# A two-layer decoder kernel: in its three attentions the transposes go ahead of the value product, and four exponentials run in a row

## The chip, the cores and the metric

The kernel runs on one core of one Trainium2 chip. A core has five engines with instruction queues of their own, which meet only through semaphores: TensorE (PE: matmuls and transposes into PSUM; its weight loads are listed as PEld), VectorE (DVE), ScalarE (ACT), GpSimd (POOL) and SyncE (SP, transfers). The metric is the device time of one execution in microseconds, lower is better.

## What is computed

A decoder of two layers on x of 8 batches x 128 tokens x 128 features, with a context of 8 x 77 x 128. Six blocks follow each other, each added to its input and normalised. Blocks 1, 2 and 5 are attentions with 16 heads of 8 features; they are what the change touches:

```python
x = _layernorm(x + _L0_attn_ref(x, ...))            # attention 1: own keys, 128 of them
x = _layernorm(x + _L0_xattn_ref(x, ctx_1024, ...)) # attention 2: 77 keys of the context
x = _layernorm(x + _L0_ffn_ref(x, ...))             # mixture of experts
x = _layernorm(x + _L1_attn_ref(x, ...))            # state space model and small attention
x = _layernorm(x + _L1_xattn_ref(x, ctx_1024, ctx_1024, mask_1x1xSxS2_bk1, ...))  # attention 5: 77 keys, masked
x = _layernorm(x + _L1_ffn_ref(x, ...))             # experts with full capacity

scores = jnp.einsum('bhqd,bhkd->bhqk', Q, K) / jnp.sqrt(jnp.float32(D_K))
scores = jnp.where(mask, -jnp.inf, scores)
attn_w = jax.nn.softmax(scores, axis=-1)
out = jnp.einsum('bhqk,bhkd->bhqd', attn_w, V)
```

## The kernel before

The three attentions use the same code, with an object `Attention` each (`at1`, `at2`, `at5`) that holds the semaphores and says which PSUM bank a step uses. The work goes batch by batch (B = 8); the 16 heads lie in four groups of 32 rows (G = 4), and a group's four heads are told apart by keys that are zero outside their head. One batch takes these steps:

- `scores(b)` (PE, L1572): query by keys for the four groups, into four banks; attention 5 writes the mask first (L1565).
- `maximum(b, g)` (DVE, L1064), four of them: the largest score of each query and head.
- `remainder(b, k)` (DVE, L1074), two of them: splits the maxima into parts that bf16 holds exactly.
- `flips(i)` (PE): up to four things into one bank: the output projection of batch i-3 (L1636), in attention 2 for i = 1 to 4 the transpose of a late query (L1640), the transpose of the maxima of batch i+1 (L1643), the transpose of the normalised values of batch i-2 (L1646). It waits for `part_ready`, that is both remainders of batch i+1, and for `normed`.
- the flips' copy (ACT, L707) takes the maxima and the values to SBUF; in attention 2 a second one (L709) takes the late query.
- `shifted(b)` (PE): keys by query once more, transposed (L1596), minus the flipped maxima (L1603); in attention 5 the masks come first (L1589). It waits until all its four banks are read, among them that of the first maximum of batch b+1, and for the flips' copy.
- `exponentials(b, groups)` (ACT, L690), four of them.
- `weigh(b)` (PE, L1625): values by exponentials, with the sums as an extra column.
- copy of the weighted values (ACT, L701), their transposes back (PE, L1674), which I call turns, then on DVE `inverse` (L1029; in attention 5 also L1033) and `normalise` (L1041).
- `residual` (DVE, L1017) adds the projection, `statistics` and `apply` (L1004) normalise, with one power on POOL between them. In attention 2 DVE also scales a late query (L1205) at the end of turns 0 to 3.

The order of each engine is written out by hand. PE's turn i is `shifted(i)`, `weigh(i-1)`, `flips(i)`, `scores(i+2)`, turns of i-1. ACT's turn i is exponentials 0 and 1 of i, copy of the weighted values of i-1, flips' copy of i, exponentials 2 and 3 of i. DVE's turn i is `residual(i-3)`, maximum 0 of i+2, `inverse(i-1)`, maximum 1, `normalise(i-1)`, maxima 2 and 3, remainder 0, `apply`, remainder 1, `statistics`. Seven banks go round in a ring (`RING_BANKS`) for scores, `flips` and `shifted`; the order of their uses is `SLOTS`. `between`, `middle`, `within` and `opening` are pieces of the neighbouring blocks that are set into chosen turns.

Of the kernel before, what the change touches and what calls it, by code (L numbers as in the profile page):

```python
# [30 lines left out]
G = 4  # L31
# [78 lines left out]
BURSTS = [("max", 0), ("flip", -1), ("max", 1)]  # L110
for _i in range(B):
    BURSTS += [("exp", _i), ("flip", _i)] + ([("max", _i + 2)] if _i + 2 < B else [])
SLOTS = [(what, i, g) for what, i in BURSTS for g in range(1 if what == "flip" else G)]
PLACE = {slot: n for n, slot in enumerate(SLOTS)}


class Attention:


    def __init__(self, sem, name, nk, scale, kM, V, Wo, XB, Xout, masked=False, late=None):  # L120
# [5 lines left out]
        self.late = late  # L126
        self.scores_ready = sem(f"{name}_scores_ready")
# [17 lines left out]
    def bank(self, what, i, g=0):  # L145

        if what == "flip" and i >= B:
            return 5 if i == B + 1 else 7
        return RING_BANKS[PLACE[what, i, g] % len(RING_BANKS)]

# [10 lines left out]
    def wait_bank(self, pe, what, i, g=0):  # L161
# [6 lines left out]
        place = PLACE[what, i, g] - len(RING_BANKS)  # L168
        if place >= 0:
            before, k, slot = SLOTS[place]  # L170
# [28 lines left out]
def _build(nc, ctx, a, out):  # L199
# [37 lines left out]
    mask8 = sb("mask8", [128, NC], U8); maskneg = sb("maskneg", [128, NC], BF16); maskrep8 = sb("maskrep8", [128, 4, NC], U8); maskrep = sb("maskrep", [128, 4, 2, NC], BF16); negkey = sb("negkey", [128, J, NC], BF16); first32 = sb("first32", [128, T], BF16); eye32 = sb("eye32", [128, 32])  # L237
# [247 lines left out]
    def _(pool):  # L485
# [23 lines left out]
        P_.memset(first32[:], 0.0)  # L509
# [144 lines left out]
    def _(act):  # L654
# [27 lines left out]
        def attention_scalar(at, between):  # L682
# [10 lines left out]
            for i in range(-1, B + 4):  # L693
                if 0 <= i < B:
                    exponentials(i, (0, 1))
# [7 lines left out]
                if i < B + 2:  # L703

                    lo, hi = (0 if i + 1 < B else T), (2 * T if i >= 2 else T)
                    act.wait_ge(at.flipped_ready, i + 2)
                    A_(flipped[:, i % 2, lo:hi], PS[:, at.bank("flip", i), lo:hi], ACT.Copy).then_inc(at.flipped_copied, 1)  # L707
                if at.late and 1 <= i <= HB:
                    A_(qT[:, HB + i - 1, :], PS[:, at.bank("flip", i), 3 * T:4 * T], ACT.Identity,  # L709
                       scale=gb2[:, 0:1], bias=gb2[:, 1:2]).then_inc(at.late, 1)  # L710
                if 0 <= i < B:
                    exponentials(i, (2, 3))
# [220 lines left out]
    def _(dve):  # L933
# [123 lines left out]
        def attention_vector(at, between, middle={}, ending=last_batches):  # L1057
# [19 lines left out]
            for i in range(-2, B):  # L1077
# [4 lines left out]
                if ahead:  # L1082
                    maximum(i + 2, 0)
                if done:
                    inverted = inverse(at, n)
                if ahead:
                    maximum(i + 2, 1)
# [1115 lines left out]
```

## Time and profile before

| | |
|---|---|
| median of 3 executions | 397.94 us (396.94 to 400.10) |
| the profiled execution | 400.24 us, span 398.4 us between its first and last instruction |
| mean granted clock of TensorE | 0.98 |
| busy share of the span | PE 90%, DVE 69%, PEld 60%, ACT 53%, POOL 37% |
| attention 1, about 14 to 66 us | PE busy 45.35 us of 52, DVE 41.36, ACT 32.02 |
| attention 2, about 74 to 115 us | PE busy 36.54 us of 41, DVE 24.08, ACT 24.32 |
| attention 5, about 253 to 303 us | PE busy 43.49 us of 50, DVE 30.41, ACT 21.63 |

The profile is one execution, times in microseconds from the first instruction. A matmul is listed from its start to its modelled end, and matmuls overlap, so a step's length is read from start to start. The granted clock is a share of full speed: 1.00 is 2.4 GHz, 0.50 is 1.2 GHz. A bracket at the end of a timeline row says how long the engine sat idle before it, and what ended that.

### The profile page before, as it was taken

What the parts mean: (1) busy time and instruction counts of PE and PEld (TensorE: products, weight loads), DVE (VectorE), ACT (ScalarE), POOL (GpSimd) and SP (SyncE); (2) the same over time, 40 slices, a digit from 0 to 9 for tenths busy, and PEclk for the clock granted to TensorE, in tenths of its full rate; (3) what the DMA queues carried; (4) which work ended last, traced back from release to release, by engine and by line L of the source; (5) the groups of instructions that cost most, each with busy time, mean ns of one, the idle gap of its engine ahead of it and who ended that gap; (6) DMA issues with size and microseconds to landing.
All of it is one profiled execution on the core that took longest, in us unless ns stands there. A gap on an engine that the chain in (4) does not pass through costs nothing.

```text
span 398.4 us, 10075 instructions
## 1 busy us (share of the span) xinstructions
PE 358.2 (90%) x4034; PEld 240.3 (60%) x4039; DVE 275.5 (69%) x712; ACT 211.1 (53%) x427; POOL 145.5 (37%) x128
## 2 busy tenths in 40 slices
PE   4988898798998989999999999699898999999991
PEld 2555565566675746566767667366664566666671
DVE  6877978736757877789899995755566445444546
ACT  2855468655674345999999951144354521222110
POOL 6939952481441420038889980200112000000002
PEclk9999999969999989999999999999999999999997
DMA  6335100000000030212223240620000000000001
GB/s 176 83 66 30 11 3 1 4 2 2 4 2 0 2 18 3 69 56 86 105 91 112 87 57 2 213 106 3 3 7 0 2 0 0 2 1 0 2 0 53
DMA packets 36810, 14.57 MB, mean 37 GB/s; under 512 B 26452, under 2 KB 34061, under 8 KB 36765
## 3 DMA queue, kind: packets, MB, share of 16 engines
q1 hardware_dynamic: 35466, 13.23, 13.7%
q10 hardware_dynamic: 1299, 0.71, 0.6%
q8 instruction: 32, 0.52, 0.6%
q14 instruction: 13, 0.11, 0.1%
HBM read 12.65 MB, written 0.57 MB: 33 GB/s over the span
## 4 chain that ended last, share of the span: by engine, by line
PE 78%; DVE 10%; ACT 6%; issue 4%; POOL 2%; POOLq 0%; DVEq 0%
PE PS L2045 10%; PE PS L2130 7%; PE PS L2134 7%; PE PS L2161 7%; PE PS L1625 6%; PE PS L1596 6%; PE PS L2032 5%; PE PS L1572 4%; PE PS L1532 4%; DVE mxp L1064 3%; PE PS L1538 2%; PE PS L1636 2%; PE PS L1837 2%; PE PS L1527 2%; PE PS L1589 1%
## 5 line engine op out<-in xcount | busy, mean ns | idle before, releaser
L690 ACT ACTIVATE att<-PS 103x384 f32<-103x384 f32 (+1 forms) x96 | 45.1, 525 | 43.7 <-PE PS L1603 43.7
L1064 DVE TENSOR_REDUCE mxp<-PS 128x4 f32<-128x308 f32 (+1 forms) x96 | 48.2, 536 | 21.0 <-PE PS L1572 20.9
L929 ACT ACTIVATE kM<-PS 128x512 f32<-128x512 f32 x32 | 19.1, 597 | 55.4 <-PE PS L2130 55.4
L533 POOL TENSOR_TENSOR rstd<-ve,neg_half 128x4 f32<-128x4 f32 x6 | 6.1, 1025 | 103.9 <-DVE ve L959 103.9
L539 POOL TENSOR_TENSOR rstd<-ve,neg_half 128x1 f32<-128x1 f32 x24 | 14.2, 593 | 77.3 <-DVE ve L1000 77.3
L1471 DVE TENSOR_TENSOR big<-kM,PS 128x512 f32<-128x512 f32 x32 | 21.9, 687 | 27.3 <-PE PS L2134 26.0
L1387 DVE TENSOR_TENSOR_SCAN big<-big,PS 128x768 f32<-128x768 f32 x22 | 38.2, 1746 | 2.5 <-PE PS L2032 2.2
L2130 PE MATMUL PS<-xT,V 128*128 128x512 f32 x64 | 33.0, 597 | 1.1 <-DVE xT L1459 0.8
L2134 PE MATMUL PS<-xT,V 128*128 128x512 f32 x64 | 32.7, 592 | 0.0
L2161 PEld LDWEIGHTS PS<-big 128*128 128x128 f32 x256 | 29.7, 192 | 3.3 <-issue 3.3
L2161 PE MATMUL PS<-big 128*128 128x128 f32 x256 | 29.7, 275 | 0.0
L895 ACT ACTIVATE att<-big,BT 128x256 f32<-128x256 f32 x64 | 27.1, 493 | 0.0
L1492 DVE SCALAR_TENSOR_TENSOR R<-PS,aff,R 128x128 f32<-128x128 f32 x56 | 15.8, 344 | 11.2 <-PE PS L2161 11.2
L578 POOL TENSOR_TENSOR hr<-hvar,half_bh 77x32 f32<-77x32 f32 (+1 forms) x5 | 22.0, 4424 | 1.8 <-DVE hvar L986 1.8
L1596 PE MATMUL PS<-qT,kM 32*103 32x128 f32 x384 | 18.5, 301 | 3.6 <-DVE mxp L1064 2.6
L2134 PEld LDWEIGHTS PS<-xT,V 128*128 128x128 f32 x64 | 12.2, 190 | 15.3 <-issue 14.8
L1625 PE MATMUL PS<-att,V 103*32 103x128 f32 x512 | 19.0, 285 | 1.2 <-issue 0.9
L1387 DVE TENSOR_TENSOR_SCAN untransposed<-untransposed,PS 128x768 f32<-128x768 f32 x10 | 17.4, 1744 | 3.5 <-PE PS L2032 3.4
L881 ACT ACTIVATE big<-big,Aneg 128x760 f32<-128x760 f32 x22 | 19.6, 915 | 0.0
L2032 PE MATMUL PS<-ident,att 128*128 128x128 f32 x128 | 19.3, 273 | 0.4 <-ACT att L895 0.4
L1518 PE MATMUL PS<-negsel,identb 128*128 128x512 bf16 x49 | 14.8, 424 | 4.7 <-DVE negsel L1116 4.4
L2130 PEld LDWEIGHTS PS<-xT,V 128*128 128x128 f32 x64 | 11.5, 190 | 12.5 <-issue 11.2
(363 smaller groups left out, 832.8 us busy)
## 6 DMA issues: line engine op xcount, KB each, us to landing
kM<-Cdram SPq DMA_DIRECT2D x6, 384.0 KB, 3.3
XH<-Cdram SPq DMA_DIRECT2D x5, 384.0 KB, 3.3
xT<-Cdram SPq DMA_DIRECT2D x5, 384.0 KB, 3.5
V<-in_L_ffn_Wg SPq DMA_DIRECT2D x1, 1024.0 KB, 5.5
V<-in_L_ffn_Wu SPq DMA_DIRECT2D x1, 1024.0 KB, 8.1
out_x<-X SPq DMA_DIRECT2D x2, 256.0 KB, 2.3
ctxN<-in_ctx ACTq DMA_DIRECT2D x1, 308.0 KB
X<-in_x ACTq DMA_DIRECT2D x1, 256.0 KB, 3.8
```

The costliest lines, as they stand in the source:

```text
L578: P_.tensor_tensor(out=hr1[0:NC, n], in0=hvar[0:NC, n], in1=half_bh[0:NC, 0:n.stop - n.start], op=ALU.pow)\
L690: A_((PTk if at.packed else PT)[0:at.kt, i % 2, g], bank4(at.bank("exp", i, g), at.kt)[:, 0:nt, :], ACT.Exp, scale=at.scale).then_inc(at.e ...
L895: ins = A_(scaled[s % 2][k], duT[:, k, :], ACT.Identity, scale=BT[:, k, s:s + 1])
L1064: V_.tensor_reduce(mxp[:, b % 3, g, 0:J], PS[:, at.bank("max", b, g), 0:J * nk].rearrange("p (j k) -> p j k", j=J), axis=AX.X, op=ALU.max) ...
L1387: V_.tensor_tensor_scan(hst[m % NHS], dA[m % NDA], dBu[m % NDB], 0.0, ALU.mult, ALU.add)\
L1596: M_(tile(b, g, k), keys, qT[rows(g), b, :], start=not at.masked, stop=False)
L1625: ins = M_(PS[32 * u:32 * u + 32, at.out_bank(b), k * T:(k + 1) * T], values[0:at.kt, lo:lo + VW], weights, start=(x == 0), stop=(x == 1))
L2032: ins = nc.tensor.transpose(dBu[n % NDB][:, 128 * k:128 * (k + 1)], scaled[s % 2][k][:, 128 * h:128 * (h + 1)], ident[:])
L2045: ins = M_(y_piece(h, lo, hi), ident[:], hC[n % NHC][:, lo:hi], start=False, stop=(n // NH == DS - 1 and (h, lo) != (0, 512)))
L2130: M_(PS[:, n % 2, :], Wg6[:, e, i * 128:(i + 1) * 128], half(xT, c), start=True, stop=True)\
L2134: M_(PS[:, 2 + n % 2, :], Wu6[:, e, i * 128:(i + 1) * 128], half(xT, c), start=True, stop=True)\
L2161: ins = M_(PS[:, 4 + (2 * e + c) % 4, b4 * D:(b4 + 1) * D], hidE[e % 2][:, i, b * T:(b + 1) * T], Wd6[:, NI * e + i, :], start=(i == 0), s ...
```

## The change

The order within a turn changes on three engines, for all three attentions alike. PE: for i < 8 `flips(i)` stands ahead of `weigh(i-1)`, and `scores(i+2)` behind it; from i = 8 on the order is as before, and ahead of each `between` a wait for `residual_ready` is added. ACT: the four exponentials of a batch run in a row, then the flips' copy (and the late query's), then the copy of the weighted values; from i = 8 on as before. DVE: maximum 1 stands ahead of `inverse`. The masks of attention 5 for the first 32 queries are written 32 columns wide instead of 128, `first32` is that much narrower, and its memset on POOL goes. The slots are computed per attention, with the same content.

```diff
--- before.py
+++ after.py
@@ -107,11 +107,14 @@
 
 
 RING_BANKS = [0, 1, 2, 3, 4, 5, 7]
-BURSTS = [("max", 0), ("flip", -1), ("max", 1)]
-for _i in range(B):
-    BURSTS += [("exp", _i), ("flip", _i)] + ([("max", _i + 2)] if _i + 2 < B else [])
-SLOTS = [(what, i, g) for what, i in BURSTS for g in range(1 if what == "flip" else G)]
-PLACE = {slot: n for n, slot in enumerate(SLOTS)}
+
+
+def slots():
+
+    bursts = [("max", 0), ("flip", -1), ("max", 1)]
+    for i in range(B):
+        bursts += [("exp", i), ("flip", i)] + ([("max", i + 2)] if i + 2 < B else [])
+    return [(what, i, g) for what, i in bursts for g in range(1 if what == "flip" else G)]
 
 
 class Attention:
@@ -124,6 +127,8 @@
         self.kt = KT if self.packed else T
         self.Wo, self.XB, self.Xout, self.masked = Wo, XB, Xout, masked
         self.late = late
+        self.slots = slots()
+        self.place = {slot: n for n, slot in enumerate(self.slots)}
         self.scores_ready = sem(f"{name}_scores_ready")
         self.max_ready = sem(f"{name}_max_ready")
         self.part_ready = sem(f"{name}_part_ready")
@@ -146,7 +151,7 @@
 
         if what == "flip" and i >= B:
             return 5 if i == B + 1 else 7
-        return RING_BANKS[PLACE[what, i, g] % len(RING_BANKS)]
+        return RING_BANKS[self.place[what, i, g] % len(RING_BANKS)]
 
     def out_bank(self, b):
 
@@ -165,9 +170,9 @@
             if i == B + 2:
                 self.wait_flip_read(pe, B)
             return
-        place = PLACE[what, i, g] - len(RING_BANKS)
+        place = self.place[what, i, g] - len(RING_BANKS)
         if place >= 0:
-            before, k, slot = SLOTS[place]
+            before, k, slot = self.slots[place]
             if before == "flip":
                 self.wait_flip_read(pe, k)
             else:
@@ -234,7 +239,7 @@
     untransposed = sb("untransposed", [128, 12 * D])
     W5 = untransposed[:, 0:4 * D].rearrange("p (i n) -> p i n", i=4)
     W5T = sb("W5T", [128, 4, D])
-    mask8 = sb("mask8", [128, NC], U8); maskneg = sb("maskneg", [128, NC], BF16); maskrep8 = sb("maskrep8", [128, 4, NC], U8); maskrep = sb("maskrep", [128, 4, 2, NC], BF16); negkey = sb("negkey", [128, J, NC], BF16); first32 = sb("first32", [128, T], BF16); eye32 = sb("eye32", [128, 32])
+    mask8 = sb("mask8", [128, NC], U8); maskneg = sb("maskneg", [128, NC], BF16); maskrep8 = sb("maskrep8", [128, 4, NC], U8); maskrep = sb("maskrep", [128, 4, 2, NC], BF16); negkey = sb("negkey", [128, J, NC], BF16); first32 = sb("first32", [128, 32], BF16); eye32 = sb("eye32", [128, 32])
     maskf = sb("maskf", [128, NC]); nmasked = sb("nmasked", [128, 1]); anykey = sb("anykey", [128, 1])
     gate3 = sb("gate3", [E0, D]); gate3T = sb("gate3T", [128, E0])
     down3 = untransposed[:, 4 * D:8 * D].rearrange("p (i n) -> p i n", i=4)
@@ -506,7 +511,6 @@
         affine(ident[:], ALU.not_equal, [[-1, 128]]).then_inc(const_ready, 1)
         pool.wait_ge(const_ready, 1)
         P_.memset(identb[:], 0.0)
-        P_.memset(first32[:], 0.0)
         P_.memset(after[:], 0.0)
         P_.memset(earlier[:], 0.0)
         P_.memset(mxp[:], 0.0).then_inc(event("mxp_zero"), 1)
@@ -692,7 +696,19 @@
 
             for i in range(-1, B + 4):
                 if 0 <= i < B:
-                    exponentials(i, (0, 1))
+                    exponentials(i, range(G))
+                def flips_out():
+                    if i < B + 2:
+
+                        lo, hi = (0 if i + 1 < B else T), (2 * T if i >= 2 else T)
+                        act.wait_ge(at.flipped_ready, i + 2)
+                        A_(flipped[:, i % 2, lo:hi], PS[:, at.bank("flip", i), lo:hi], ACT.Copy).then_inc(at.flipped_copied, 1)
+                    if at.late and 1 <= i <= HB:
+                        A_(qT[:, HB + i - 1, :], PS[:, at.bank("flip", i), 3 * T:4 * T], ACT.Identity,
+                           scale=gb2[:, 0:1], bias=gb2[:, 1:2]).then_inc(at.late, 1)
+
+                if i < B:
+                    flips_out()
                 if 0 <= i - 1 < B:
 
                     act.wait_ge(at.pv_done, i)
@@ -700,16 +716,8 @@
                         act.wait_ge(at.out_ready, i - 1)
                     A_(outT[:], PS[:, at.out_bank(i - 1), 0:2 * T].rearrange("p (k t) -> p k t", k=2), ACT.Copy)\
                         .then_inc(at.outT_copied, 1)
-                if i < B + 2:
-
-                    lo, hi = (0 if i + 1 < B else T), (2 * T if i >= 2 else T)
-                    act.wait_ge(at.flipped_ready, i + 2)
-                    A_(flipped[:, i % 2, lo:hi], PS[:, at.bank("flip", i), lo:hi], ACT.Copy).then_inc(at.flipped_copied, 1)
-                if at.late and 1 <= i <= HB:
-                    A_(qT[:, HB + i - 1, :], PS[:, at.bank("flip", i), 3 * T:4 * T], ACT.Identity,
-                       scale=gb2[:, 0:1], bias=gb2[:, 1:2]).then_inc(at.late, 1)
-                if 0 <= i < B:
-                    exponentials(i, (2, 3))
+                if i >= B:
+                    flips_out()
                 if i in between:
                     between[i]()
 
@@ -1081,10 +1089,9 @@
                     residual(at, r)
                 if ahead:
                     maximum(i + 2, 0)
+                    maximum(i + 2, 1)
                 if done:
                     inverted = inverse(at, n)
-                if ahead:
-                    maximum(i + 2, 1)
                 if done:
                     normalise(at, n, inverted)
                 if i in middle:
@@ -1153,7 +1160,7 @@
             V_.tensor_scalar(maskrep[:], maskrep8[:].rearrange("p c (o k) -> p c o k", o=1).to_broadcast([128, 4, 2, NC]), MASKED,
                              None, ALU.mult)
             step(V_.tensor_reduce(eye32[:], ident[:].rearrange("p (g r) -> p r g", g=G), axis=AX.X, op=ALU.add))
-            V_.tensor_copy(first32[:, 0:32], eye32[:])
+            V_.tensor_copy(first32[:], eye32[:])
             step(V_.tensor_reduce(nmasked[:], mask8[:], axis=AX.X, op=ALU.add))
             step(V_.tensor_scalar(anykey[:], nmasked[:], float(NC), None, ALU.is_lt))
 
@@ -1582,11 +1589,11 @@
 
                 if at.masked:
                     for c in range(4):
-                        q = slice(32 * c, 32 * c + 32) if c else slice(0, T)
+                        q = slice(32 * c, 32 * c + 32)
                         for k, lo in enumerate(at.tiles):
                             for g in range(G):
                                 keys = maskrep[rows(g), c].rearrange("p r n -> p (r n)")[:, lo % NC:lo % NC + KT]
-                                M_(tile(b, g, k)[:, q], keys, first32[rows(g), 0:q.stop - q.start], start=(c == k == 0), stop=False)
+                                M_(tile(b, g, k)[:, q], keys, first32[rows(g), 0:32], start=(c == k == 0), stop=False)
                 for k, lo in enumerate(at.tiles):
                     for g in range(G):
                         if at.packed:
@@ -1658,16 +1665,18 @@
                     shifted(i)
                 if i == 0:
                     opening[4]()
+                if i < B:
+                    flips(i)
                 if 0 <= i - 1 < B:
                     weigh(i - 1)
-                if i < B + 3:
+                if i + 2 < B:
+                    scores(i + 2)
+                if B <= i < B + 3:
                     flips(i)
                 if i in middle:
 
                     pe.wait_ge(at.exp_ready, G * min(i, B))
                     middle[i]()
-                if i + 2 < B:
-                    scores(i + 2)
                 if 0 <= i - 1 < B:
                     pe.wait_ge(at.outT_copied, i)
                     for k in range(2):
@@ -1678,6 +1687,7 @@
                 if i in between:
 
                     pe.wait_ge(at.exp_ready, G * B)
+                    pe.wait_ge(at.residual_ready, B - 3)
                     between[i]()
 
             if last_wait:
```

## Rows read from the trace of the kernel before

**Rows 1.** Waits of PE, all of the span: us in total, times, longest.

```profile
PE PS L1596 <- DVE mxp L1064: 6.8, 10, 0.9
```

**Rows 2.** Chain of waits, attention 1: start, us, what held the end.

```profile
20.78 0.14 issue
...
29.43 1.16 PE PS L1572 x8
30.59 0.70 DVE mxp L1064
```

**Rows 3.** Timeline, one turn of attention 1: start, us, engine, line, out<-in, idle before.

```profile
30.59 0.69 DVE L1064 TENSOR_REDUCE mxp<-PS 128x4 f32<-128x512 f32 x1 [0.64 <-PE PS L1572]
...
33.02 1.08 PE L1625 MATMUL PS<-att,big 128*32 128x128 f32 x32
...
33.41 0.38 DVE L1074 TENSOR_TENSOR mxp<-mxp 128x16 f32<-128x16 f32 x2
...
34.04 0.33 PE L1643 MATMUL PS<-ident,mxp 128*128 128x128 f32 x1
```

**Rows 4.** Timeline of PE, attention 1: first and last scores, last turns.

```profile
24.53 1.14 PE L1572 MATMUL PS<-big,qT 32*128 32x512 f32 x8
...
50.39 1.14 PE L1572 MATMUL PS<-big,qT 32*128 32x512 f32 x8
...
53.98 1.08 PE L1625 MATMUL PS<-att,big 128*32 128x128 f32 x32
...
56.26 0.50 PE L1596 MATMUL PS<-qT,big 32*128 32x128 f32 x8 [0.26 <-ACT flipped L707]
...
57.75 1.08 PE L1625 MATMUL PS<-att,big 128*32 128x128 f32 x32
...
61.27 0.49 PE L1636 MATMUL PS<-Wo,flipped 128*128 128x128 f32 x2
```

**Rows 5.** Timeline of ACT, attentions 1 and 2: two exponentials, a copy.

```profile
54.12 1.08 ACT L690 ACTIVATE att<-PS 128x512 f32<-128x512 f32 x2 [2.26 <-PE PS L1603]
55.12 0.38 ACT L701 ACTIVATE outT<-PS 128x256 f32<-128x256 f32 x1
...
104.33 0.87 ACT L690 ACTIVATE att<-PS 103x384 f32<-103x384 f32 x2 [1.52 <-PE PS L1603]
```

**Rows 6.** Timeline, attention 2, turns 1, 3 and 4.

```profile
79.40 0.28 DVE L1205 TENSOR_TENSOR qc<-qc,hr 128x128 f32<-128x128 f32 x1
...
79.46 1.94 PE L1625 MATMUL PS<-att,V 103*32 103x128 f32 x32
...
93.02 0.29 DVE L1017 TENSOR_TENSOR R<-XB,PS 128x128 f32<-128x128 f32 x1 [2.20 <-ACT qT L709]
...
95.03 1.08 PE L1625 MATMUL PS<-att,V 103*32 103x128 f32 x32
...
96.10 0.29 DVE L1205 TENSOR_TENSOR qc<-qc,hr 128x128 f32<-128x128 f32 x1
```

**Rows 7.** Timeline, attention 5, turn 2.

```profile
269.97 0.39 DVE L1074 TENSOR_TENSOR mxp<-mxp 128x16 f32<-128x16 f32 x2
...
270.09 1.08 PE L1625 MATMUL PS<-att,V 103*32 103x128 f32 x32
```

**Rows 8.** Groups by line and shape: mask matmuls; busy us, mean ns.

```profile
L1589 PE MATMUL PS<-first,maskrep 32*103 32x32 bf16 x288 | 4.8, 192 | 0.0
L1589 PE MATMUL PS<-first,maskrep 32*103 32x128 bf16 x96 | 3.1, 227 | 2.7 <-DVE mxp L1064 1.9 <-ACT flipped L707 0.8
```

**Rows 9.** Timeline, the start.

```profile
2.28 0.20 POOL L509 MEMSET first<- 128x128 bf16 x1
...
3.18 0.29 DVE L1114 TENSOR_REDUCE headmask<-ident 128x4 f32<-128x128 f32 x1 [3.18 <-POOL mxp L512]
```

**Rows 10.** Busy time by stretch: length; PE, PEld, DVE, ACT, POOL; clock; DMA share, GB/s.

```profile
80.00:85.00 5.00, 4.87 (x56) 2.89 (x52) 1.46 (x5) 2.12 (x6) 5.00 (x3) 0.50 0.00 0
253.00:258.00 5.00, 3.40 (x51) 1.33 (x51) 2.89 (x14) 0.71 (x2) 1.01 (x1) 1.00 1.04 346
```

## Prediction

> **What bounds the kernel now.** I read the granted clock first (0.98 on the one core), then PE's waits, then the chain of waits, then the timeline of PE, DVE and ACT through the three attentions. The change touches nothing else but one memset at the start.
>
> PE's waits: inside the attentions the longest total is `shifted` (L1596) waiting for the maxima of DVE, 6.8 us in 10 waits, none over 0.9 [rows 1]. The chain shows why. In attention 1 it goes round as scores (PE), first maximum (DVE, 30.59, 0.70 us), `shifted`, `weigh`, `flips`, scores again [rows 2]. So per batch PE is the bound, with one hole in which the first maximum is made. A second loop runs beside it: scores, all four maxima and two remainders on DVE, `flips`, scores. Its length shows in the timeline of attention 1: the first maximum of a batch starts at 30.59, the second remainder ends at 33.41+0.38 = 33.79, and `flips`, which needs it, starts at 34.04. Between 33.02 and 34.04 PE does `weigh` [rows 3]. The reader is to see that `weigh` is what PE does while DVE finishes the remainder: `shifted` ends, `weigh` starts at 33.02, the remainder is 0.77 us from its end.
>
> **The change, part by part.**
>
> *1. `flips(i)` ahead of `weigh(i-1)` on PE.* `flips(i)` transposes the maxima of batch i+1, so it waits for both remainders of that batch. Scores of batch i+1 are issued one turn earlier, behind the same `weigh`. Now the order is scores, `shifted`, `flips`, `weigh`, scores; the two loops are no longer side by side: the DVE loop gets `weigh` in series. Queued behind the waiting `flips` on PE are `weigh(i-1)`, scores(i+2) and the transposes of the weighted values; DVE waits for scores, ACT for `weigh`.
>
> Attention 1, from scores to scores: 1.16 us from the scores' start (29.43) to the first maximum (30.59) and 0.14 us from a remainder's end to PE's start [rows 2]; 3.20 us from the first maximum to the end of the second remainder, 0.33 us of transposes, 1.01 us of `weigh` (33.02 to 34.04) [rows 3]: 5.84 us. The first of five such steps has no inverse and no normalisation between its maxima (0.29 us less), the last has an `apply` between its remainders (0.14 us more). Sum 5 x 5.84 - 0.15 = 29.05 us. Before, scores(2) started at 24.53 and scores(7) at 50.39, so the same five steps took 25.86 us [rows 4]. **+3.2 us.**
>
> Attention 2 has shorter maxima (308 columns), but in turns 1 to 4 `flips` also turns a late query, which DVE scales behind the remainders. Here I count the wait itself: end of DVE's last piece, plus latency, less the end of `shifted` (where `weigh` starts now), less 0.32 us for the projection that `flips` does first from turn 3. Turn 1: 79.40+0.28+0.06-79.46 = 0.28 us; turn 4, the largest: 96.10+0.29+0.06-95.03-0.32 = 1.1 us [rows 6]. The same sum gives 0.30, 0.50 and 0.50 for turns 2, 3 and 5; together 2.7 us. Something comes back: at 93.02 DVE's `residual` starts 2.20 us idle, held by ACT's late query copy, and holds the first maximum back [rows 6]. With `flips` 1.01 us before the scores that hold is gone, 0.4 us in each of two turns. **+1.9 us.**
>
> Attention 5 has its mask matmuls in `shifted`, which makes `shifted` longer and gives DVE more time. Turn 2: the remainder ends at 269.97+0.39 = 270.36, `weigh` starts at 270.09, so the wait is 0.41 us [rows 7]; turns 3, 4 and 5 by the same sum 0.09, 0 and 0.23. **+0.7 us.**
>
> *2. Four exponentials in a row on ACT, then the flips' copy, then the weighted values' copy.* In the middle of an attention this is covered: the next consumer of either copy stands behind scores, 1 us or more later. The cover is gone at the last two turns, where no scores follow. Turn 6: the copy of the weighted values starts when `weigh(5)` is done, which itself waited; in attention 1 that is 2.5 us behind the end of `shifted` (wait 1.05, transposes 0.31, then 1.14 as from `weigh` at 53.98 to the copy at 55.12), then 0.38 for the copy, 0.14 to PE, and an estimated 0.37 for two transposes (by the 0.33 of one in [rows 3]): `shifted(7)` starts 3.4 us behind, against 56.26-53.98 = 2.28 before [rows 4, 5]: +1.1 us. Attention 2 by the same sum +0.9, attention 5 +0.6. Turn 7: four exponentials take 1.08+2x0.49 = 2.1 us in attention 1 and 0.87+2x0.38 = 1.6 in the others [rows 5]; then the copies, the transposes, then `weigh(7)`, which stands behind them on PE: 4.2 us from the end of `shifted(7)` to the next `flips`, against 61.27-57.75 = 3.52 before [rows 4]: +0.7; in the two others 3.7 against 3.3: +0.4 each. **+4.1 us over the three.**
>
> *3. Masks in 32 columns instead of 128 (attention 5).* The wide form takes 227 ns on average, the narrow 192 [rows 8]. In a batch 12 wide ones run four abreast, so three rounds of 0.035 us: 0.1 us a batch. From below it is worth nothing, if weight loads set the pace; from above 0.15 us, three whole rounds of the 0.05 us at which the 48 go. It counts only in turns where `flips` does not wait for DVE, some three of eight: **-0.3 us** (0 to -0.5).
>
> *4. Memset of `first32` gone from POOL.* DVE's first instruction waits for POOL's `mxp` memset until 3.18 [rows 9]; the memset removed stands before it and takes 0.20 us with some overlap. **-0.15 us** (0 to -0.2).
>
> *5. At nothing:* the second maximum ahead of the inverse (same DVE work; it covers a later transpose of the weighted values), the extra wait for `residual_ready` ahead of `between` (the `flips` before it needs a normalisation which DVE does behind that residual), the slots made per attention (same order, same banks). Without its cover each costs at most one DVE piece, 0.3 us, a few times: under 1 us together.
>
> Sum: 3.2 + 1.9 + 0.7 + 4.1 - 0.3 - 0.15 = **+9.4 us**. The profiled execution took 400.24 us, so it would take 409.7. The median of the runs shown is 397.94, 2.3 us below it; I put the sum on the median: **407.4 us**.
>
> **TensorE's clock.** The row of 80 to 85 us shows the granted clock at 0.50, the lower level of 1.2 GHz; from 253 to 258, with PE busy only 3.40 us of 5, it stayed at 1.00, the level of 2.4 GHz [rows 10]. At the lower level `weigh` takes 1.94 instead of 1.08 us [rows 6]; 5 us at half rate cost up to 2.5 us. The changed attention 1 would have PE busy about 4.35 of 5.84 us, 3.7 of 5, above a window that kept the clock, so I count nothing for it and make it a rival. The Trainium skill, "TensorE: Matmul & The Clock Gate", section "A second HAM failure mode: psum-queue depth-cycling", says that short idle gaps between groups of matmuls can make the clock swing between its levels. By that page each swing would add 2.5 us to the sum; by the row of 253 to 258 it need not come.
>
> **Rivals.**
> *A lower clock on top.* One more stretch as in [rows 10], 2.5 us, gives 409.9; two give 412.4. For it: attention 2 already has such a stretch, and the change adds holes of 0.3 to 1.1 us to every turn. Against: the idler window at 253 us kept the clock. The stretch of before may also vanish, 2.5 us the other way: 404.9.
> *Only the ends cost.* If in the middle turns DVE's loop is shorter than its rows say, parts 2 to 4 remain: 4.1-0.45 = +3.7, 401.6 us. Against: the parts of that loop are all data dependences, measured in place.
> *Not slower.* PE idles before `shifted` anyway, and `weigh` next to scores could fill this hole. The place is the wait of `flips` for the second remainder. It decides the other way only if the remainder ends before `shifted` does: 0.77 us earlier in attention 1, 0.3 to 1.1 in attention 2, 0.4 in attention 5. Then the masks (eight times 0.1), the held residual (0.8) and the memset remain, with the ends covered: -1.7, 396.2 us. For it: in attention 5 three of five waits are under 0.25 us. Against: DVE cannot begin before scores end, and nothing in the change moves scores forward.
>
> **Chances.** Forecast 0.62 (its own range 404.9 to 409.9: the old stretch gone, or a longer one), lower clock on top 0.17, only the ends 0.13, not slower 0.08. A measurement of this kernel tells about 1% from no change, so 394.0 and 401.9 are the bounds. Slower: forecast, lower clock and over half of "only the ends", 0.87. Faster: a small part of "not slower", 0.03. Same: the rest, 0.10. The range of 8 in 10 goes from "only the ends", 401.8, to a first added stretch at the lower clock and part of a second, 412.5.
>
> **What would show it.** In the profile of the changed kernel: PE's waits should name `flips` (the transpose of `mxp`) waiting for DVE's remainder, some 0.6 to 0.9 us a turn in attention 1, where before there was none; from scores to scores about 5.85 us in attention 1; `shifted` still waiting for the first maximum; the transposes of the weighted values at turns 6 and 7 waiting for ACT's copy. It would be wrong if `flips` starts without a wait, if scores to scores stays near 5.2 us in attention 1, or if the attentions are longer in stretches at clock 0.50 instead of by waits.

## The result and the profile after

| | |
|---|---|
| median after, 4 executions | 411.58 us (408.97 to 411.79) |
| median before beside it, 4 executions | 397.76 us (396.94 to 400.10) |
| ratio after to before, 95% interval | 1.0294 (1.0253 to 1.0334): slower |
| the profiled execution after | 411.61 us, span 409.8 us (before 400.24, 398.4) |
| busy share of the span | PE 88%, DVE 68%, PEld 59%, ACT 51%, POOL 36% |

The forecast was 407.4 us, with 401.8 to 412.5. The ratio stands for 11.7 us on 397.76; the two medians lie 13.8 us apart, and the profiled execution after has a late start of 1.96 us, which the last section shows. The forecast's sum was 9.4. Three executions in the sets below were in a second, much slower state (1974.85 us of the changed kernel with ACT as before, 609.26 and 606.60 us of before): the ratios leave them out, the medians count them. PE's busy time is nearly the same (360.9 us, before 358.2): what is added is waiting. The waits of PE in the changed kernel (us in total, times, longest):

```profile
PE PS L1603 <- DVE mxp L1072: 7.4, 13, 0.9
PE PS L1650 <- DVE mxp L1082: 5.4, 10, 1.0
...
PE PS L1683 <- ACT outT L717: 3.4, 6, 0.7
PE PS L1647 <- DVE qc L1212: 3.1, 4, 1.1
```

Lines have moved: L1603 is `shifted` (before L1596), L1650 the transpose of the maxima in `flips` (L1643), L1647 that of the late query (L1640), L1683 the turns (L1674), L1072 `maximum`, L1082 `remainder`. The reader is to see that the wait of `shifted` for the first maximum is nearly as it was (6.8 us in [rows 1], 7.4 now), and that three waits are new or were small: `flips` for the second remainder, 5.4 us, and for the late query, 3.1 us, and the turns for ACT's copy, 3.4 us.

Where they lie is in the timeline of the changed kernel: one turn of attention 1, its end, a mask block of attention 5, and at the top three rows from the start of the kernel.

```profile
3.03 0.29 DVE L1121 TENSOR_REDUCE headmask<-ident 128x4 f32<-128x128 f32 x1 [3.03 <-POOL mxp L516]
...
4.31 0.87 DVE L962 BATCH_NORM_STATS2 st<-X 128x6 f32<-128x128 f32 x4 [0.20 <-DMA X<-in_x]
...
8.27 1.12 PE L1534 MATMUL PS<-ident,XH 128*128 128x128 f32 x4 [0.45 <-DVE XH L974]
...
31.91 1.14 PE L1579 MATMUL PS<-big,qT 32*128 32x512 f32 x8
...
33.12 1.29 DVE L1072 TENSOR_REDUCE mxp<-PS 128x4 f32<-128x512 f32 x2 [1.22 <-PE PS L1579]
...
34.33 0.25 DVE L1037 RECIPROCAL rs<-PS 128x16 f32<-128x16 f32 x1
...
34.61 0.29 DVE L1049 TENSOR_TENSOR oN<-PS,rs 128x128 f32<-128x128 f32 x1
...
36.13 0.38 DVE L1082 TENSOR_TENSOR mxp<-mxp 128x16 f32<-128x16 f32 x2
...
36.66 0.30 PE L1650 MATMUL PS<-ident,mxp 128*128 128x128 f32 x1 [1.03 <-DVE mxp L1082]
...
37.00 1.08 PE L1632 MATMUL PS<-att,big 128*32 128x128 f32 x32
38.01 1.14 PE L1579 MATMUL PS<-big,qT 32*128 32x512 f32 x8
...
61.21 1.08 PE L1632 MATMUL PS<-att,big 128*32 128x128 f32 x32
62.79 0.44 PE L1683 MATMUL PS<-ident,outT 128*128 128x128 f32 x2 [0.50 <-ACT outT L717]
63.16 0.50 PE L1603 MATMUL PS<-qT,big 32*128 32x128 f32 x8
...
67.36 0.44 PE L1683 MATMUL PS<-ident,outT 128*128 128x128 f32 x2 [0.52 <-ACT outT L717]
67.73 1.08 PE L1632 MATMUL PS<-att,big 128*32 128x128 f32 x32
68.74 0.49 PE L1643 MATMUL PS<-Wo,flipped 128*128 128x128 f32 x2
...
278.34 0.76 PE L1596 MATMUL PS<-first,maskrep 32*103 32x32 bf16 x48 [0.39 <-DVE mxp L1072]
278.92 0.48 PE L1603 MATMUL PS<-qT,kM 32*103 32x128 f32 x8
```

In [rows 3] PE did `weigh` while DVE finished the remainder. Here PE stands still for 1.03 us until 36.66, and `weigh` follows at 37.00. From scores (31.91) to scores (38.01) 6.10 us pass.

### The profile page after: what moved, and what is told of

It is laid out like the page before. It is cut to its first block, busy times and chain, and to the rows that moved or that the text cites. A ratio compares the mean times of both kernels' runs of the same rounds, so it can differ in the third digit from the quotient of the medians.

```text
span 409.8 us, 10069 instructions
## 1 busy us (share of the span) xinstructions
PE 360.9 (88%) x4039; PEld 240.5 (59%) x4039; DVE 278.2 (68%) x712; ACT 208.6 (51%) x427; POOL 145.7 (36%) x127
## 4 chain that ended last, share of the span: by engine, by line
PE 71%; DVE 15%; ACT 6%; issue 5%; POOL 1%; DMA 1%; POOLq 0%; DVEq 0%
PE PS L2055 10%; PE PS L2140 7%; PE PS L2144 7%; DVE mxp L1072 7%; PE PS L2171 7%; PE PS L1632 5%; PE PS L1579 5%; PE PS L2042 5%; PE PS L1539 4%; PE PS L1545 3%; PE PS L1603 2%; PE PS L1534 2%; PE PS L1847 2%; ACT att L694 1%; PE PS L1650 1%
## 5 line engine op out<-in xcount | busy, mean ns | idle before, releaser
L694 ACT ACTIVATE att<-PS 103x384 f32<-103x384 f32 (+1 forms) x96 | 42.6, 529 | 57.7 <-PE PS L1610 57.7
L1072 DVE TENSOR_REDUCE mxp<-PS 128x4 f32<-128x308 f32 (+1 forms) x96 | 47.5, 542 | 26.9 <-PE PS L1579 26.8
L1603 PE MATMUL PS<-qT,kM 32*103 32x128 f32 x384 | 17.8, 291 | 2.9 <-DVE mxp L1072 2.7
L1525 PE MATMUL PS<-negsel,identb 128*128 128x512 bf16 x54 | 16.5, 436 | 4.3 <-DVE negsel L1123 4.3
L2042 PEld LDWEIGHTS PS<-ident,att 128*128 128x128 f32 x128 | 15.3, 141 | 5.7 <-issue 3.6
```

Source lines behind the costliest of these rows:

```text
L694: A_((PTk if at.packed else PT)[0:at.kt, i % 2, g], bank4(at.bank("exp", i, g), at.kt)[:, 0:nt, :], ACT.Exp, scale=at.scale).then_inc(at.e ...
L1072: V_.tensor_reduce(mxp[:, b % 3, g, 0:J], PS[:, at.bank("max", b, g), 0:J * nk].rearrange("p (j k) -> p j k", j=J), axis=AX.X, op=ALU.max) ...
L1603: M_(tile(b, g, k), keys, qT[rows(g), b, :], start=not at.masked, stop=False)
L2042: ins = nc.tensor.transpose(dBu[n % NDB][:, 128 * k:128 * (k + 1)], scaled[s % 2][k][:, 128 * h:128 * (h + 1)], ident[:])
```

## Where the time went, and eleven experiments

Each kernel is read by the same six lengths from its timeline of PE: for each attention the **middle** (from the start of scores(2) to the start of scores(7), five steps) and the **end** (from there to the start of the projection in `flips(8)`, the part in which no scores follow). In attention 5 both are read from the first product of query and keys, behind the masks that scores write first. A star marks a length into which a stretch at a lower granted clock falls.

| kernel | median us | ratio (95%) | middles 1, 2, 5 | ends 1, 2, 5 |
|---|---|---|---|---|
| before | 397.76 | | 25.86, 24.96*, 26.93 | 10.88, 9.31, 10.50 |
| after | 411.58 | 1.0294 (1.0253 to 1.0334) | 29.61, 25.53, 27.85 | 12.64, 10.60, 11.46 |
| PE order alone | 409.63 | 1.0234 (1.0187 to 1.0281) | 28.87, 26.16, 27.43* | 12.19, 10.66, 11.30 |
| ACT order alone | 401.52 | 1.0032 (1.0011 to 1.0052) | 26.01, 22.41, 27.20 | 12.35, 10.20, 11.41 |
| DVE order alone | 399.11 | 1.0000 (0.9965 to 1.0036) | 26.29, 22.46, 27.20 | 10.92, 9.31, 10.51 |
| masks and memset alone | 399.73 | 1.0007 (0.9980 to 1.0033) | 25.85, 22.37, 26.86* | 10.89, 9.46, 10.46 |
| after, split flips | 404.89 | 1.0123 (1.0021 to 1.0225) | 26.59, 22.62, 28.01* | 12.35, 10.36, 11.53 |
| after, DVE as before | 409.47 | 1.0246 (1.0150 to 1.0342) | 28.87, 24.79, 27.65 | 12.45, 10.42, 11.34 |
| after, ACT as before | 411.63 | 1.0309 (1.0212 to 1.0406) | 29.61, 26.90, 26.81* | 12.38, 10.84, 11.41 |
| after, once more | 411.21 | 1.0293 (1.0211 to 1.0374) | 31.20*, 25.52, 27.58 | 12.64, 10.60, 11.46 |
| after, ends as before | 407.69 | 1.0214 (1.0174 to 1.0254) | 29.61, 25.52, 27.11* | 10.92, 9.31, 10.46 |
| split flips, ACT as before | 400.72 | 1.0047 (1.0014 to 1.0081) | 26.58, 24.39*, 27.12 | 11.39, 9.83, 10.96 |
| split flips, ends as before | 399.24 | 1.0006 (0.9977 to 1.0036) | 26.58, 22.62, 27.39 | 10.92, 9.31, 10.46 |

The ratios are against before in executions made beside them; its median there was 399.81 us for the four with one part alone, 401.03 for split flips to "once more", and 399.67 for the last three. Attention 2's middle of before is 22.4 us without its stretch at the lower clock, by the three kernels that do not touch PE's order. With that, after against before is 3.75 + 3.13 + 0.92 us in the middles and 1.76 + 1.29 + 0.96 in the ends, 11.8 us. That agrees with the ratio's 11.7.

**One part alone.** The first four kernels are before with one part of the change. In the diffs here and below, "..." marks a cut and the comments are added.

*PE's order* (with the added wait for `residual_ready`):

```diff
+                if i < B:
+                    flips(i)
                 if 0 <= i - 1 < B:
                     weigh(i - 1)
-                if i < B + 3:
+                if i + 2 < B:
+                    scores(i + 2)
+                if B <= i < B + 3:
                     flips(i)
...
-                if i + 2 < B:
-                    scores(i + 2)
...
```

> The kernel before with PE's order alone changed (flips ahead of weigh, the added wait for the residual). Theory A, the loop over DVE gets weigh in series: flips waits for the second remainder; from scores(2) to scores(7) in attention 1 about 29 us instead of 25.9, shifted(7) 3.4 us behind the end of shifted(6) instead of 2.3 since weigh(5) is late; +7 to +9 us in all. Theory B, the copies that ACT does later are the cause: from scores to scores as before, +0 to +2 us. Theory C, TensorE's clock at its lower level is the cause: scores to scores as before outside a stretch at granted clock 0.50.

```profile
PE PS L1643 <- DVE mxp L1074: 3.9, 9, 0.8
PE PS L1676 <- ACT outT L701: 2.5, 5, 0.5
PE PS L1640 <- DVE qc L1205: 1.9, 3, 0.9
```

These are waits of PE in that kernel; L1643 and L1640 are `flips`, which in before waited for the maxima 0.5 us in all. 409.63 us, 9.8 more than the 399.81 beside it and more than the 7 to 9 expected: this part alone brings most of the loss. In attention 1 the middle took 28.87 us, 3.01 more than before; the prediction's sum had 3.2. The three ends are 3.46 us longer too, with ACT's order untouched.

*ACT's order:*

```diff
-                    exponentials(i, (0, 1))
+                    exponentials(i, range(G))
...
+                if i < B:
+                    flips_out()     # flips' copy, late query's copy
                 if 0 <= i - 1 < B:  # then the copy of the weighted values
...
```

> The kernel before with ACT's order alone changed (four exponentials, flips' copy, weighted values' copy). Theory A: in the middle turns nearly covered, 0.1 to 0.3 us a turn, since the transposes of the weighted values wait for the copy; in the last two turns shifted(7) about 3.3 us behind the end of shifted(6) in attention 1 instead of 2.3, then 4.2 to the next flips instead of 3.5; +3 to +5 us in all. Theory B: nearly all of the loss is here, +9 us or more. Theory C: about 0 outside a stretch at clock 0.50.

The end of attention 1 in that kernel, timeline of ACT and PE:

```profile
54.55 2.06 ACT L690 ACTIVATE att<-PS 128x512 f32<-128x512 f32 x4 [2.62 <-PE PS L1607]
56.47 0.42 ACT L701 ACTIVATE flipped<-PS 128x256 f32<-128x256 f32 x1
56.73 0.43 ACT L713 ACTIVATE outT<-PS 128x256 f32<-128x256 f32 x1
...
57.22 0.44 PE L1678 MATMUL PS<-ident,outT 128*128 128x128 f32 x2 [1.09 <-ACT outT L713]
```

The copy of the weighted values comes behind four exponentials and a copy, and the turns wait 1.09 us for it. The middles stay within 0.3 us of before's; the three ends are 3.27 us longer. The ratio, 1.0032, shows only part of that. The ten executions of this kernel had a mean granted clock of 0.990 on average, the 25 of before beside them 0.985. Where the clocks are alike, at 0.989 and 0.990, four executions of it took 401.16 to 402.76 us and six of before 397.60 to 398.53, on average 401.74 and 398.12: 3.6 us, where the six lengths add up to 3.7.

*DVE's order:* `maximum(i + 2, 1)` ahead of `inverse`.

> The kernel before with DVE's order alone changed (second maximum ahead of the inverse). If inverse and normalise, now back to back, wait for each other, the time from the first maximum to the end of the second remainder grows from 3.20 to about 3.4 us in attention 1; flips has some 0.1 us of slack there, so 0 to +1 us in all. If the order is free, 0.

399.11 us, no difference that can be told; the middle of attention 1 is 0.43 us longer. The chain from the first maximum to the end of the second remainder grew: 30.65 to 34.04 in its timeline, 3.39 us, against 3.20 in [rows 3]; in before's PE order `weigh` covers most of that.

*Masks 32 columns wide, memset gone:*

> The kernel before with the masks 32 columns wide and the memset of first32 gone. If a wide mask matmul costs 0.035 us more and PE is the bound, -0.1 us in each of eight turns of attention 5 and -0.15 us at the start: -0.5 to -1 us. If weight loads set the pace of the masks and the start waits for the load of x, 0.

399.73 us, no difference. The mask matmuls now take 202 ns on average; [rows 8] had 192 and 227.

**Which wait of `flips` it is.** Split flips: the changed kernel with only the projection and the transpose of the normalised values ahead of `weigh`, and the two transposes that need DVE's late results behind it.

```diff
                 if i < B:
-                    flips(i)
+                    flips(i, True, i + 1 >= B)   # projection, normalised values
                 if 0 <= i - 1 < B:
                     weigh(i - 1)
+                if i + 1 < B:
+                    flips(i, False, True)        # late query, maxima
                 if i + 2 < B:
                     scores(i + 2)
```

> The changed kernel, but of flips only the projection and the transpose of the normalised values go ahead of weigh; the late query and the transpose of the maxima, which wait for DVE's remainders, go behind it. Theory A (the DVE loop has weigh in series): scores(2) to scores(7) in attention 1 back from 29.6 to about 26 us, PE's wait for the remainder gone, what is left is ACT's late copies in the last two turns; some 7 us less than the changed kernel, +3 to +5 us over the kernel before. If it is the position of flips as such or the order of ACT and DVE: still +9 us or more.

One turn of attention 1, timeline of PE:

```profile
33.06 0.33 PE L1649 MATMUL PS<-ident,oN 128*128 128x128 f32 x1
33.31 1.08 PE L1632 MATMUL PS<-att,big 128*32 128x128 f32 x32
34.33 0.33 PE L1656 MATMUL PS<-ident,mxp 128*128 128x128 f32 x1
34.59 1.14 PE L1579 MATMUL PS<-big,qT 32*128 32x512 f32 x8
```

No row has a bracket: nothing waits. `weigh` starts at 33.31 and the maxima are there when it ends. The middle of attention 1 falls from 29.61 to 26.59 us, that of attention 2 from 25.53 to 22.62; attention 5's (28.01) can't be compared, as the stretch at a lower clock falls into it. So the cost of the middles is the wait for DVE ahead of `weigh`, and not `flips` ahead of `weigh` as such. The ends stay long, and the time is 404.89 us.

**DVE's order under the changed PE order.** The changed kernel with `inverse` back between the two maxima:

> The changed kernel with DVE's old order (inverse between the first and second maximum). In the changed kernel first maximum to end of second remainder takes 3.39 us in attention 1, against 3.20 before; here it should be 3.20 again, and since flips waits for it, every step from scores to scores is 0.15 to 0.2 us shorter: -2 to -2.5 us against the changed kernel over 15 turns. If the inverse then has to wait for the late transposes of the weighted values, less than that or 0.

```profile
31.41 0.69 DVE L1072 TENSOR_REDUCE mxp<-PS 128x4 f32<-128x512 f32 x1 [1.22 <-PE PS L1580]
32.01 0.25 DVE L1037 RECIPROCAL rs<-PS 128x16 f32<-128x16 f32 x1
32.18 0.63 DVE L1072 TENSOR_REDUCE mxp<-PS 128x4 f32<-128x512 f32 x1
32.72 0.28 DVE L1049 TENSOR_TENSOR oN<-PS,rs 128x128 f32<-128x128 f32 x1
32.91 1.28 DVE L1072 TENSOR_REDUCE mxp<-PS 128x4 f32<-128x512 f32 x2
34.23 0.39 DVE L1082 TENSOR_TENSOR mxp<-mxp 128x16 f32<-128x16 f32 x2
```

409.47 us, 2.1 less than after, but 1.7 less than the changed kernel once more (411.21), which ran beside it, and the intervals of the two ratios overlap: by the times alone it isn't clear of the noise. The lengths show it. The chain is 31.41 to 34.62, 3.21 us, where after has 33.12 to 36.51, 3.39. Attention 1's middle gives back 0.74 us, attention 2's 0.74, attention 5's 0.20, the ends 0.49: 2.2 us.

**ACT's order under the changed PE order.** The changed kernel with ACT as before:

> The changed kernel with ACT's old order (two exponentials, weighted values' copy, flips' copy, two exponentials). Theory A: scores to scores as in the changed kernel, about 29.6 us for the five in attention 1; in the last turn 0.3 us instead of 0.6 over before; -1 us or so against the changed kernel, +10 us over before. Theory B: most of the loss gone.

411.63 us: nothing comes back. The ends give 0.07 us, and attention 2's middle is 1.37 us longer. (Attention 5's is 1.04 us shorter, 0.68 of it in the last step, where the changed kernel has a stall without a wait; see below.) This timeline of it shows why attention 2's grew:

```profile
105.28 0.38 ACT L705 ACTIVATE outT<-PS 128x256 f32<-128x256 f32 x1 [2.23 <-PE PS L1628]
105.56 0.38 ACT L711 ACTIVATE flipped<-PS 128x256 f32<-128x256 f32 x1
105.83 0.46 ACT L713 ACTIVATE qT<-PS,gb 128x128 f32<-128x128 f32 x1
...
107.35 0.48 PE L1599 MATMUL PS<-qT,kM 32*103 32x128 f32 x8 [1.03 <-DVE mxp L1068]
```

ACT copies the weighted values first, so it waits for `weigh`, which now comes late. Behind it stand flips' copy and the late query's copy (105.83; in after 104.05), DVE's `residual` waits for the latter, the first maximum for `residual`, and `shifted` 1.03 us for the maximum (0.38 in after). ACT's new order takes this away; under the new PE order it costs nothing.

**The clock at the start.** The changed kernel unaltered, once more:

> The changed kernel unchanged, once more. In its first profile TensorE's clock was low in the first 15 us, which put scores(2) of attention 1 at 26.5 instead of 24.5 us; the kernel before had its low stretch in attention 2. If where such a stretch falls is chance, this profile has it elsewhere or not at all, with scores to scores in attention 1 the same 29.6 us; if the change puts it at the start, scores(2) is at 26.5 again.

411.21 us. Its scores(2) started at 24.61, where the first profile of the changed kernel has 26.49 and before 24.53 [rows 4]. The expectation puts the late start down to a low clock; the rows of the first profile show the clock at 1.00 there (last section). This profile lost the time elsewhere. Busy time by stretch (columns as in [rows 10]):

```profile
35.00:40.00 5.00, 4.39 (x48) 2.31 (x50) 1.12 (x2) 1.70 (x5) 5.00 (x2) 0.66 0.58 33
```

Two steps of attention 1 took 7.01 and 6.65 us instead of 6.10 and 5.99, which makes its middle 31.20.

**The ends.** The changed kernel with turns 6 and 7 in the order of before on PE and ACT:

```diff
-                if i < B:
+                if i < B - 2:
                     flips(i)
...
-                if B <= i < B + 3:
+                if B - 2 <= i < B + 3:
                     flips(i)
```

On ACT, likewise, `range(G)` becomes `(0, 1)` in these turns, and exponentials 2 and 3 come last.

> The changed kernel, with turns 6 and 7 of each attention (where no scores follow) in the order of before on PE and ACT: weigh ahead of flips, copy of the weighted values and flips' copy between the exponentials. Theory A (the order of the last two turns itself costs, as the prediction's part 2 says): from the start of the last scores of attention 1 to the first scores of attention 2 it goes from 20.16 back to 18.4-18.7 us, attention 5's end by about 1.0, attention 2's by about 1.0; together -3.5 to -4 against the changed kernel, some 407.5-408. Theory B (the end is longer because the middle turns hand it a later state, as it was 19.70 with the PE order alone too): it stays at 19.7 or more and the time at 410.5-411.5.

407.69 us, 3.9 less than after. The ends are 10.92, 9.31 and 10.46 us, those of before, and the middles of attentions 1 and 2 are unchanged (attention 5's is 0.74 us shorter, without the stall in its last step). So the order of the last two turns itself costs; the middle hands it nothing.

Split flips with ACT's order as before:

> The changed kernel with only the projection and the transpose of the normalised values ahead of weigh (maxima and late query behind it), and ACT's order as before. If ACT's order is what is left of the loss in the kernel with the split flips (404.89), the end of attention 1 goes from 19.86 to 18.4-18.7 us and the time to that of before, within 1 us of it. If the PE order of the last two turns (flips whole ahead of weigh) lengthens the ends by itself, the end of attention 1 stays near 19.7 and the time 3-4 us above before.

400.72 us, 1.1 above the 399.67 beside it; but at clocks of 0.989 to 0.991 five executions took 400.62 us on average and three of before 397.73, 2.9 less. The ends are still 1.49 us longer than before's, 0.5 each: in turn 7, where no maxima are left, `flips` still goes whole ahead of `weigh(6)`.

Split flips, with turns 6 and 7 as before:

> The changed kernel with split flips in turns 0 to 5 and the order of before in turns 6 and 7 on PE and ACT; ACT's row of four exponentials stays in the middle turns. Both costs named (wait ahead of weigh, ends) are gone: the time of before within 1 us, 0 to -0.5 if the narrow masks' 0.03 us a turn can be seen. If the middle turns of ACT's order cost by themselves, 1-2 us above before, seen in the steps from scores to scores (26.0 in attention 1 with ACT's order alone, 25.86 before).

399.24 us against 399.67, ratio 1.0006 (0.9977 to 1.0036): both costs are gone as far as the ratio tells. The lengths still have 0.72 us in attention 1's middle, of which DVE's order alone had 0.43, about 0.2 in attention 2's and 0.46 in attention 5's; and where the clocks are alike it is slower: at 0.993 and 0.994 four executions took 398.17 us on average, four of before 396.84, 1.3 us less. Nothing of the change is left that helps, and a version that beats before did not come out of it.

## Point by point

**The bound and the main term: right.** *1, attention 1* was +3.2 us; PE's order alone measured +3.01, and with DVE's new order 3.75. `flips` waits for the remainder (0.55, 1.03, 0.43, 0.53, 0.66 and 0.66 us in turns 1 to 6), as the wait was predicted; scores to scores was to be 5.84 us and is 5.98 to 6.12 in four of five steps.

*1, attention 2* was +1.9 us and is +3.13. The waits in the changed kernel are 0.53, 1.00, 0.49, 1.12 and 0.43 us, 3.57 in all, where the prediction had 0.28, 0.30, 0.50, 1.1 and 0.50:

```profile
87.30 0.30 PE L1647 MATMUL PS<-ident,qc 128*128 128x128 f32 x1 [0.53 <-DVE qc L1212]
...
92.37 0.30 PE L1647 MATMUL PS<-ident,qc 128*128 128x128 f32 x1 [1.00 <-DVE qc L1212]
...
97.45 0.33 PE L1647 MATMUL PS<-ident,qc 128*128 128x128 f32 x1 [0.49 <-DVE qc L1212]
...
103.18 0.33 PE L1647 MATMUL PS<-ident,qc 128*128 128x128 f32 x1 [1.12 <-DVE qc L1212]
...
108.22 0.33 PE L1650 MATMUL PS<-ident,mxp 128*128 128x128 f32 x1 [0.43 <-DVE mxp L1082]
```

The two that are far off are turns 1 and 2, read from [rows 6] and beside them, where PE ran at the lower clock. There `shifted`, whose end stands in the sum, took 1.34 us (78.12 to 79.46 in the timeline of before) and 1.83 (84.11 to 85.94); at full clock it takes 1.09 (89.13 to 90.22). The differences, 0.25 and 0.74 us, are nearly what the two waits are longer than predicted, 0.25 and 0.70. The starts in the timeline of before:

```profile
78.12 0.48 PE L1596 MATMUL PS<-qT,kM 32*103 32x128 f32 x8 [0.72 <-DVE mxp L1064]
...
84.11 0.77 PE L1596 MATMUL PS<-qT,kM 32*103 32x128 f32 x8
...
85.94 1.08 PE L1625 MATMUL PS<-att,V 103*32 103x128 f32 x32
...
89.13 0.48 PE L1596 MATMUL PS<-qT,kM 32*103 32x128 f32 x8 [0.53 <-ACT att L690]
...
90.22 1.08 PE L1625 MATMUL PS<-att,V 103*32 103x128 f32 x32
```

That turns 3 to 5 agree is in part luck: DVE's new order, counted at nothing, is in the measured waits, and with DVE as before they are 0.30, 0.94 and 0.24 us. DVE's order has 0.74 us in this middle; with DVE as before it is 24.79, +2.4. The hold of `residual` went as predicted, though ACT's new order is needed for it.

*1, attention 5* was +0.7 and is +0.92, in part by luck: the first four steps are 1.27 us longer, and the last is 0.34 shorter because before's has a stall of 0.94 us within `weigh` that no wait explains (at 287.49). The changed kernel has such stalls too, of 0.19 us (274.46) and 0.27 (298.24). What they come from is open, and the term is not settled more closely.

*2, the ends* were +4.1 us over the three and are +4.01, by attention 1.76 (predicted 1.8), 1.29 (1.3) and 0.96 (1.0). The size is right, in part by luck: 0.49 us of it goes with DVE's new order, which the term did not have. The name is half right: the prediction counted the late `weigh(5)` in turn 6, but filed the whole term under ACT's order. PE's order alone costs 3.46 us, ACT's alone 3.27, both 4.01; with ACT as before nearly all of it stays. They are two ways of delaying the same copy of the weighted values: it comes behind `weigh`, which PE holds back for the remainder, or behind two more exponentials.

*3, masks* were -0.3 us. The block of 48 mask matmuls takes 0.58 us (278.34 to 278.92) and took 0.61 (273.31 to 273.92 in the timeline of before): 0.03 us a batch, not 0.10, near the bound "worth nothing, if weight loads set the pace".

*4, memset* was -0.15 us. DVE does start at 3.03 instead of 3.18 [rows 9], but its first `BATCH_NORM_STATS2` then waits 0.20 us for the load of x, and starts at 4.31 (4.19 before). It is worth nothing.

**The step that was mis-sized** is *5*, the edits at nothing: "the second maximum ahead of the inverse" was to be the same DVE work. It adds 0.18 us to the chain from the first maximum to the second remainder, and part 1 had just put that chain on the path: 2.2 us by the lengths of the kernel with DVE as before, where all of *5* was bounded at "under 1 us together". The term was costed with the cover of the old order, which the change itself removes.

**The rivals.** "Not slower" and "only the ends" are out: `flips` waits 14 times for DVE. "A lower clock on top" did not come as told. The stretches of 30 to 65 us and 80 to 120 us of the changed kernel are at 1.00 throughout, though PE waits in each turn. The Trainium skill, "TensorE: Matmul & The Clock Gate", section "A second HAM failure mode: psum-queue depth-cycling", tells of a kernel whose clock swung between its two levels because PE idled briefly between groups of matmuls; the profile of the changed kernel shows none of that in its attentions, that of "once more" one stretch at 0.66, and before, without these gaps, one at 0.50 [rows 10]. Holes in the turns alone do not bring a lower clock here.

**Why the number was low.** The measured lengths give 11.8 us where the sum had 9.4. Attention 1 is 0.55 us over its term, attention 2 1.23, attention 5 0.22, the ends 0.09 under, and masks and memset, 0.45 in the sum, gave next to nothing. DVE's order is 1.5 us of that in attentions 1 and 2. The median stands another 1.8 us above 407.4 + 2.4. That is about the late start of 1.96 us in the profiled execution (411.61 us), which no term has; two of the other three took 411.54 and 411.79 us, the third 408.97, and whether those two started late as well is not shown.

## What to carry over

Before an instruction is moved ahead of another on an in-order engine, ask what it waits for: it may be the work that it passes that covers the wait, and then only the parts with early operands can move (split flips). Once a chain has lost its cover, cost every edit on that chain again, also those that were free. Look at the turns where the pipeline drains by themselves: here they were a third of the loss, and two edits that each delay the same copy don't add up.

## What the hardware showed that was not expected

A dependent DVE instruction right behind its source started later here than an independent one. Behind the reciprocal, a maximum starts 0.17 us later (32.01 to 32.18), the normalisation that waits for it 0.28 us later (34.33 to 34.61 in after's timeline); two maxima in a row take 1.21 us, 1.14 with another instruction behind each (0.60 + 0.54). That is the 0.18 us of part 5. The kind of instruction does not decide it: the maximum behind the reciprocal starts 0.08 us before the end listed for it (32.26), and the normalisation behind a maximum 0.09 us before that one's end (32.81; it starts at 32.72), but right behind the reciprocal that it reads 0.03 us after its end (34.58). The Trainium skill, "VectorE: DVE Perf Modes", section "The DRAIN you can't avoid", says of eight copies in a row that a semaphore after each costs nothing extra; here the instruction that waits for the result of the one ahead pays 0.11 us.

PE can run slowly while the granted clock is shown as 1.00. In the first profile of the changed kernel the transposes at 8.27 take 1.12 us for four (0.66 in before) and scores(2) comes 1.96 us late, while the clock of 5 to 20 us is shown as 1.00; the kernel with ACT as before has the same late start (26.51), the others don't. These four transposes take 1.0 us or more in nine of the thirteen profiles; in the two with the late start the slowness lasts, and the eight matmuls that follow from 11.06 take 4.90 us (3.64 in before). What makes them slow is open. The stretches with a lower clock lie elsewhere in each profile: 80 to 85 us in before (0.50), 35 to 40 in "once more" (0.66), 260 to 265 with split flips (0.50), none but the last instants with ACT's order alone. In before, executions with a mean clock of 0.994 took 396.31 and 396.54 us, one of 0.978 took 401.52. So one profile can be 2 to 2.6 us off in a single stage (1.96 at the start here, 2.56 in before's attention 2), and stages are to be compared by their undisturbed lengths.
